# A two-layer decoder's state space scan: two states on the partition halves, 64-column state sums, and copied step sizes

## The reference

```python
xz = x @ W_in;  xc, z = split(xz)
xc = silu(causal_conv4(xc) + conv_b)
dt_r, Bm, Cm = split(xc @ W_xproj)            # 16, 16, 16 columns
dt = softplus(dt_r @ W_dt + b_dt)
A = -exp(A_log)                               # 512 channels x 16 states
h_t = h_{t-1} * exp(dt_t * A) + (dt_t * xc_t) * Bm_t
y_t = sum_n h_t[:, n] * Cm_t[n]
y = (y + xc * D) * silu(z)
out = y @ W_out                               # added to the residual
```

## Time and profile before

| what | us |
|---|---|
| median of three runs | 3156.37 (3152.83 to 3161.01) |
| the profiled execution's own time | 3155.42 |
| its span, first to last instruction | 3153.9 |
| Mamba stage: first scan to last finish | 39.77 to 1019.4 |
| VectorE busy in 38 to 1018 us | 917.3 of 980 |
| TensorE busy in the same stretch | 851.6 of 980 |
| mean granted TensorE clock, whole span | 0.956 |

### The profile page before, as it was taken

How to read it: one execution, slowest core, us unless ns; L and a number is a source line. 1 busy time by engine, 2 the same in 40 slices (tenths; PEclk the granted TensorE clock), 3 DMA queues, 4 the chain that set the end, 5 groups by cost and what they waited for, 6 DMA issues and landing times. The chain is left out here.

```text
span 3153.9 us, 41299 instructions
## 1 busy us (share of the span) xinstructions
PE 2825.9 (90%) x14210; PEld 1841.1 (58%) x14210; DVE 2063.7 (65%) x3705; ACT 1471.9 (47%) x2768; POOL 1510.8 (48%) x1192
## 2 busy tenths in 40 slices
PE   6898988988986877899999999988878999999998
PEld 2343343433432664555556555556657888888887
DVE  7899999999999744577777777658862222222221
ACT  5667666676763400366666666645531111111111
POOL 5788787888886544133433343256751111111111
PEclk8999999999999878999999999989988999999999
DMA  7135044053150054213232222211116665566662
GB/s 237 48 114 162 21 143 144 18 162 121 41 172 0 28 166 150 82 32 82 60 88 58 67 59 59 65 44 35 51 66 211 203 190 184 184 189 202 205 189 61
DMA packets 283854, 346.31 MB, mean 110 GB/s; under 512 B 85787, under 2 KB 238551, under 8 KB 283591
## 3 DMA queue, kind: packets, MB, share of 16 engines
q1 hardware_dynamic: 260399, 310.17, 31.8%
q0 software_dynamic: 16704, 27.21, 3.7%
q10 hardware_dynamic: 6544, 6.30, 0.7%
HBM read 234.69 MB, written 107.95 MB: 109 GB/s over the span
## 5 line engine op out<-in xcount | busy, mean ns | idle before, releaser
L542 POOL TENSOR_TENSOR mb_drive<-mb_dtx,mb_b_rep 128x1024 f32<-128x1024 f32 x255 | 597.2, 2358 | 181.9 <-DVE mb_pD L439 89.0
L853 PE MATMUL mb_pY<-mb_hc,ident 128*128 128x512 f32 x1024 | 501.6, 615 | 57.1 <-DVE mb_hc L456 56.8
L1986 DVE TENSOR_REDUCE at_nm_of<-at_pS 128x2 f32<-128x256 f32 (+1 forms) x630 | 383.3, 635 | 113.0 <-PE at_pS L1976 57.4
L3161 POOL DMA_INDIRECT out<-et_y,et_to x71 | 112.0, 1577 | 661.0 <-DVE et_y L3215 406.7
L3205 DVE TENSOR_TENSOR et_mT<-et_silu,et_pU 128x512 f32<-128x512 f32 (+1 forms) x160 | 100.2, 627 | 470.7 <-ACT et_silu L3176 470.7
L3176 ACT ACTIVATE et_silu<-et_pG 128x512 f32<-128x512 f32 (+1 forms) x160 | 87.9, 549 | 652.6 <-PE et_pU L3237 652.6
L853 PEld LDWEIGHTS mb_pY<-mb_hc,ident 128*128 128x128 f32 x1024 | 189.7, 194 | 328.7 <-issue 184.4
L598 ACT ACTIVATE mb_pD<-mb_dt,mb_a_neg 128x512 f32<-128x512 f32 x384 | 259.6, 688 | 154.6 <-DVE mb_hc L456 143.0
L439 DVE TENSOR_TENSOR_SCAN mb_pD<-mb_pD,mb_drive 128x1024 f32<-128x1024 f32 x128 | 292.8, 2288 | 43.0 <-ACT mb_pD L596 40.5
L445 DVE TENSOR_TENSOR_SCAN mb_pD<-mb_pD,mb_carried,mb_drive 128x512 f32<-128x512 f32 x256 | 313.8, 1269 | 8.0 <-ACT mb_pD L598 8.0
L456 DVE TENSOR_TENSOR mb_hc<-mb_pD,mb_c_rep 128x1024 f32<-128x1024 f32 x256 | 308.1, 1204 | 1.0 <-PE mb_pY L853 1.0
(11 more groups left out here) (491 smaller groups left out, 4986.2 us busy)
## 6 DMA issues: line engine op xcount, KB each, us to landing
t_wg<-in_t_wgT SPq DMA_DIRECT2D x40, 1024.0 KB, 6.1
t_wu<-in_t_wuT SPq DMA_DIRECT2D x40, 1024.0 KB, 9.0
t_wd<-in_t_wdT SPq DMA_DIRECT2D x40, 1024.0 KB, 11.3
mb_b_rep<-mb_rows SPq DMA_DIRECT2D x64, 512.0 KB, 5.6
mb_c_rep<-mb_rows SPq DMA_DIRECT2D x64, 512.0 KB, 4.9
t_h_sorted<-blank SPq DMA_DIRECT2D x6, 4160.0 KB, 19.9
t_h_sorted<-blank SPq DMA_DIRECT2D x18, 1170.0 KB, 6.3
t_h_sorted<-blank SPq DMA_DIRECT2D x12, 1040.0 KB, 5.8
```

Of the source, the lines that this page charges most:

```text
L542: nc.gpsimd.tensor_tensor(drive[G % RINGS][:, :, :], dtx[:, m, :].unsqueeze(1).to_broadcast([P, 2, CH]), b_rep[:, 2 * j:2 * j + 2, :], ALU ...
L853: last = nc.tensor.matmul(pY[:, :], K.ident[:, :], hc[G % RINGS][:, k, :], start=False, stop=(j == PAIRS - 1 and k == 1))
L1986: nc.vector.tensor_reduce(nm_of[t % 2][:, w0 // 512, sides[0]:sides[0] + m, qb], score_bank(t, k)[:, 0:m * w].rearrange("p (a w) -> p a w" ...
```

## The change

Channel halves and states change places. A tensor's partitions 0 to 63 now hold state 2j and partitions 64 to 127 state 2j+1, and the two slots k of the free dimension hold the channels k*64 to k*64+63 of tile m. An item has the same 256 rows of 512 as before.

- The step sizes are needed in that layout on both partition halves, so SyncE copies `dt` and `dtx` after GpSimd has made them to `dt2` and `dtx2` (three buffers, `TWINS = 3`), eight transfers of 64 x 512 (128 KB) for each tile (`twins`). Decays read `dt2`, drives read `dtx2`.
- B and C rows are read as two transfers of 64 partitions each (128 KB), each row to one half, and are shared by both slots.
- `state_sum` uses `fold` (128 x 64, two identities one above the other): slot k sums the two halves into PSUM partitions k*64 to k*64+63. The skip term is split in the same way.
- On SyncE the copies of tile 0 stand behind the B and C rows of j = 2, those of tiles 1 and 2 behind j = 7, then `fill_rows`, then those of tile 3.
- GpSimd runs `step_sizes` of the next chunk's tile 0 ahead of the drive of s = 29 and no longer of s = 31.
- `magnitude` on ScalarE waits for the copies in place of the drives. A_log is laid out anew on the host (`twin_rows`).

```diff
+    HP = P // 2
+    TWINS = 3
-        a_neg = sb("a_neg", [P, ME, NST])
+        a_neg = sb("a_neg", [P, ME, 2, PAIRS])
+        fold = sb("fold", [P, HP])
-        b_rep, c_rep = sb("b_rep", [P, NST, CH]), sb("c_rep", [P, NST, CH])
+        dt2, dtx2 = sb("dt2", [P, TWINS, 2, CH]), sb("dtx2", [P, TWINS, 2, CH])
+        b_rep, c_rep = sb("b_rep", [P, PAIRS, CH]), sb("c_rep", [P, PAIRS, CH])
...
+            def twins(ch, m):
+                nth = ch * ME + m
+                q = nth % TWINS
+                for made, to, s_made, s_to, s_used, per in ((dt, dt2, s_dt, s_dt2, s_dec, 2), (dtx, dtx2, s_dtx, s_dtx2, s_drv, 1)):
+                    eng.wait_ge(s_made, nth + 1)
+                    if nth >= TWINS:
+                        eng.wait_ge(s_used, (nth - TWINS + 1) * PAIRS * per)
+                    for k in range(2):
+                        for h in range(2):
+                            eng.dma_start(to[h * HP:(h + 1) * HP, q, k, :], made[k * HP:(k + 1) * HP, m, :]).then_inc(s_to[q], 16)
...
-                    eng.dma_start(b_rep[:, 2 * j:2 * j + 2, :], rows_dram[ch % 2][2 * j:2 * j + 2, :].partition_broadcast(P)).then_inc(s_b[j], 16)
+                    for h in range(2):
+                        eng.dma_start(b_rep[h * HP:(h + 1) * HP, j, :], rows_dram[ch % 2][2 * j + h, :].partition_broadcast(HP)).then_inc(s_b[j], 16)
...
+                    if j == 2:
+                        twins(ch, 0)
+                twins(ch, 1)
+                twins(ch, 2)
                 fill_rows(K, eng, K.h1_sorted, ch, NCH, s_fill)
+                twins(ch, 3)
...
+        def drive_of(unit, ch, m, j, r):
+            return unit.tensor_tensor(drive[r][:, :, :], dtx2[:, (ch * ME + m) % TWINS, :, :],
+                                      b_rep[:, j, :].unsqueeze(1).to_broadcast([P, 2, CH]), ALU.mult)
...
-                nc.vector.tensor_tensor(hc[r][:, :, :], pD[r][:, :, :], c_rep[:, 2 * j:2 * j + 2, :], ALU.mult).then_inc(s_hc, 1)
+                nc.vector.tensor_tensor(hc[r][:, :, :], pD[r][:, :, :], c_rep[:, j, :].unsqueeze(1).to_broadcast([P, 2, CH]), ALU.mult).then_inc(s_hc, 1)
...
+            nc.vector.tensor_tensor(fold[:, :], K.ident[:, 0:HP], K.ident[:, HP:P], ALU.add).then_inc(s_fold, 1)
...
-                    if s == 31 and ch + 1 < NCH:
+                    if s == 29 and ch + 1 < NCH:
                         step_sizes(eng, nc.gpsimd, ch + 1, 0)
...
                 if ch > 0:
-                    eng.wait_ge(s_drv, (ch - 1) * ITEMS + (m + 1) * PAIRS)
+                    twin_made(eng, s_dt2, (ch - 1) * ME + m)
+                    twin_made(eng, s_dtx2, (ch - 1) * ME + m)
...
-                    nc.tensor.matmul(pY[:, :], skip[:, m, :], xc(ch, m), start=True, stop=False)
+                    for k in range(2):
+                        nc.tensor.matmul(pY[k * HP:(k + 1) * HP, :], skip[:, m, k * HP:(k + 1) * HP], xc(ch, m), start=True, stop=False,
+                                         skip_group_check=True)
                 eng.wait_ge(s_hc, G + 1)
                 for k in range(2):
-                    last = nc.tensor.matmul(pY[:, :], K.ident[:, :], hc[G % RINGS][:, k, :], start=False, stop=(j == PAIRS - 1 and k == 1))
+                    last = nc.tensor.matmul(pY[k * HP:(k + 1) * HP, :], fold[:, :], hc[G % RINGS][:, k, :], start=False, stop=(j == PAIRS - 1),
+                                            skip_group_check=True)
```

More of the change, by code:

```diff
@@ L288, in mamba @@
             sem(n) for n in ("dec", "drv", "scan", "keep", "hc", "y", "fin", "rows", "fill"))
+        s_dt2, s_dtx2 = [sem(f"dt2_{q}") for q in range(TWINS)], [sem(f"dtx2_{q}") for q in range(TWINS)]
+        s_fold = sem("fold")
         s_b = [sem(f"b{j}") for j in range(PAIRS)]
@@ L321, in _ @@
                 loads.append((dst[:, :], io[name].rearrange("(m p) -> p m", p=P)))
-            loads += [(a_neg[:, :, :], io["mb_A_log"].rearrange("(m p) n -> p m n", p=P)),
+            loads += [(a_neg[:, :, :, :].rearrange("p m k j -> p (m k j)"), io["mb_A_log"]),
                       (w_x[:, :, :], io["mb_w_x"].rearrange("(m p) n -> p m n", p=P)),
@@ L349, in _, with twin_made @@
             for j in range(PAIRS):
-                eng.wait_ge(s_b[j], 16 * NCH)
-                eng.wait_ge(s_c[j], 16 * NCH)
-        ALL_IN = 16 * 7
+                eng.wait_ge(s_b[j], 32 * NCH)
+                eng.wait_ge(s_c[j], 32 * NCH)
+            for q in range(TWINS):
+                uses = len(range(q, NCH * ME, TWINS))
+                eng.wait_ge(s_dt2[q], 64 * uses)
+                eng.wait_ge(s_dtx2[q], 64 * uses)
+        ALL_IN = 16 * 7
+        def twin_made(eng, s_to, nth):
+            eng.wait_ge(s_to[nth % TWINS], 64 * (nth // TWINS + 1))
+        def drive_of(unit, ch, m, j, r):
+            return unit.tensor_tensor(drive[r][:, :, :], dtx2[:, (ch * ME + m) % TWINS, :, :],
+                                      b_rep[:, j, :].unsqueeze(1).to_broadcast([P, 2, CH]), ALU.mult)
         def normalise(eng, unit, ch):
@@ L426, in first_drive @@
             def first_drive():
[L427 to L430, removed]
+                twin_made(eng, s_dtx2, 0)
+                eng.wait_ge(s_b[0], 32)
+                drive_of(nc.vector, 0, 0, 0, 0).then_inc(s_drv, 1)
             def scans(G):
@@ L538, in drives @@
                 if m == 0:
-                    eng.wait_ge(s_b[j], 16 * (ch + 1))
+                    eng.wait_ge(s_b[j], 32 * (ch + 1))
                 if G >= RINGS:
                     eng.wait_ge(s_scan, 2 * (G - RINGS) + 2)
-                nc.gpsimd.tensor_tensor(drive[G % RINGS][:, :, :], dtx[:, m, :].unsqueeze(1).to_broadcast([P, 2, CH]),
-                                        b_rep[:, 2 * j:2 * j + 2, :], ALU.mult).then_inc(s_drv, 1)
+                drive_of(nc.gpsimd, ch, m, j, G % RINGS).then_inc(s_drv, 1)
             inverse_deviation(0)
@@ L582, in decay @@
                 r = G % RINGS
-                scale = a_neg[:, m, 2 * j + k:2 * j + k + 1]
+                scale = a_neg[:, m, k, j:j + 1]
+                step = dt2[:, (ch * ME + m) % TWINS, k, :]
                 if k == 0:
                     if j == 0:
-                        eng.wait_ge(s_dt, ch * ME + m + 1)
+                        twin_made(eng, s_dt2, ch * ME + m)
                     if G == RINGS - 1:
@@ L871, in _ @@
             eng.wait_ge(s_diag, ME * TAPS + ME)
+            eng.wait_ge(s_fold, 1)
             for i in range(NCH):
@@ L3295, in layout, with twin_rows @@
     same = lambda n: np.ascontiguousarray(np.asarray(inputs[n]))
+    def twin_rows(n):
+        a = np.asarray(inputs[n])
+        a = a.reshape(-1, 2, P // 2, a.shape[1] // 2, 2)
+        return np.ascontiguousarray(np.transpose(a, (4, 2, 0, 1, 3)).reshape(P, -1))
     return {
```

26 lines of the change are left out of this document (13 added, 13 removed).

## The result

Against the kernel before, over eight runs of each on one chip, the changed kernel takes 1.0034 times as long, 95% interval 1.0023 to 1.0045 (medians 3165.1 and 3154.6 us, +10.6 us; forecast +12.5 us). The profiled execution's own time is 3171.3 us, the longest of the eight. Beside each stands the stage itself in the one profiled execution of the run. In the kernel before its first scan starts at 39.77 us and its last `finish` at 1018.70 us; after, at 47.13 and 1029.95 us (+11.3).

What follows compares the result with a forecast made beforehand. VectorE was taken as the bound, its 893 us of scans and weighings unchanged, only some 62 us of waits to be won. The terms 17.9 + 4.2 - 9.6 = +12.5 us on 3155.4 gave 3168 us, range 3152 to 3187.

Steps and rivals of the forecast that it cites:

- the likeliest case: Whole kernel: GpSimd's stall at chunk ends and a later start outweigh the relief of TensorE; 3168 us, chance 0.50.
- relief and stall about cancel: Rival, same mechanisms at the kind ends: sums save 0.8 us or more, start costs 3; +8.8 us, 3164 us, chance 0.22.
- Part 1, the size for one sum: TensorE's state sum: two halves side by side take 1.1 to 1.3 us in place of 1.91, saving 0.6.
- Part 1, what reaches the end: VectorE's waits: 8.4 of 11.2 us in `finish` and 1.2 us in chunk 0 are won, -9.6 us in all.
- Part 2: Step sizes at s = 29: GpSimd stands still for ScalarE's logarithm, drives queue behind it; +17.9 us over seven boundaries.
- Part 3, the start: First copies of dt and dtx, covered by nothing: scan 3 starts at 55.9 us against 51.82, +4.2 us (3 to 6).
- Part 3, the boundaries: Copies at chunk boundaries land at 405.2 to 407.4 us, before item 32's drive at 408.5: covered, 1 to 3 us to spare.
- the halves don't overlap: Rival on TensorE's state sums: halving gives nothing and the switches cost some 5 us; 3183 us, chance 0.06.
- Faster: Rival: TensorE's relief moves ScalarE's whole chain, most decay waits go, 40 of 62 us recovered; 3138 us, chance 0.12.
- The lower clock: Rival: TensorE, idle for longer, drops to the 1.2 GHz level, a late matmul at each boundary; 3195 us, chance 0.05.
- Late copies: Rival: copies land late at chunk boundaries, 3 us at each of seven; 3189 us, chance 0.05.

Runs made afterwards that it cites:

- a_s31: The changed kernel with the step sizes back at s = 31: ratio 1.0000 to the kernel before, last finish at 1019.61 us.
- b_s29: The kernel before with only the next chunk's tile 0 step sizes moved from s = 31 to s = 29: ratio 1.0069, last finish at 1038.66 us.
- a_wide: The changed kernel with full-width state sums again, step sizes at s = 29: ratio 1.0073 to the kernel before, last finish at 1046.66 us.
- a_wide31: The changed kernel with full-width state sums and step sizes back at s = 31: ratio 1.0045 to the kernel before, last finish at 1030.32 us.
- m_rows: The changed kernel with step sizes at s = 31 and each pair of B or C rows read by one transfer: ratio 1.1238 to the kernel before.
- a_warm: The changed kernel with step sizes at s = 31 and a zero-weight matmul ahead of each state sum: ratio 1.0133 to the kernel before, last finish 1059.35 us.

## Why the prediction was right, and where it was not

The time came out within 2 us of the forecast (+10.6 against +12.5), and the mechanisms of the likeliest case are there: the stall of GpSimd ahead of drive 29, the overlapping halves, the late start. That it came so close is in part luck, since errors in the terms cancel. The interval of the ratio, +7 to +14 us, also holds the +8.8 of *relief and stall about cancel*; what speaks against that case are its terms, not the time. The steps:

- **Part 1, the size for one sum.** 1.1 to 1.3 us and a saving of 0.6 were forecast. A sum takes 1.01. Beside a convolution, which is slowed by 0.19, the saving is 3.43 - 2.92 = 0.51 us, and beside PROJ it is 0.91. The 0.1 to 0.2 us for each change of form were right. The base of 1.91 us was not a plain one: between convolutions the same sum took 1.72. Next to PROJ the kernel before paid for a change of form already.
- **Part 1, what reaches the end.** -9.6 us was forecast, and -10.7 measured at s = 31. The waits in `finish` gave 9.1 us of it (12.9 to 3.8) where 8.4 was forecast. The 5.33 us wait of chunk 0 became 5.01, not 4.1. The sum took VectorE's pitch as 3.49 us, from durations; by their starts, two scans without a wait are 3.32 us apart in an even chunk (395.26 and 398.58 in the kernel after). TensorE's 3.43 us for a state sum and a convolution is above that, so it could fall behind in dense stretches, and the forecast saw that only in `finish`.
- **Part 2.** +17.9 us forecast; +18.9 measured alone, 17.7 of it in the waits from scan 29 on. The reading of the earlier trace rows held at both kinds of chunk end; scan 29 waited 4.1 to 5.5 us, where 2.8 to 5 was said. Together with the rest of the change it cost 10.3 us. The step that failed is that the terms were added as if each were free of the others. At the chunk ends the stall swallows waits that are there without it: 22.4 us in a_s31, against 17.7 in the kernel before.
- **Part 3, the start.** +4.2 us (3 to 6) forecast, and scan 0 at 43 to 45 us; it came at 47.13, scan 3 7.7 us later than before, the first `finish` 6.8 (84.14 to 90.93). The mis-sized term is SyncE's issue, taken at 0.43 us. Twenty issues take 12.7 us (31.31 to 44.00) and not 8.6: 4.1 us.
- **Part 3, the boundaries.** Forecast as covered, and they were.

By the path before, b_s29, a_wide, after, the terms are +20.0 (1.05 of it ahead of the first scan), +8.0 and -16.7, together +11.3. By the path before, a_wide31, a_s31, after they are +11.6, -10.7 and +10.3. The forecast had +17.9 for the move, +4.2 for the copies and -9.6 for the halves. So the sum was closer than its terms on either path: by the first the start was too small by 3 to 4 us and part 1's gain too small by 7; by the second the copies were too small by 7 and the move too large by 8.

Of the rivals, *the halves don't overlap* is ruled out by the state sums. *Faster*, by way of ScalarE, is ruled out too: 21.1 us of decay waits remain at s = 29, but 39.0 at s = 31, where 40.5 were before, so part 1 did not take them away; the stall only renamed them. *Relief and stall about cancel* wanted 0.8 us or more from each sum and 3 us at the start; beside a convolution a sum gave 0.51, and the first scan came 7.4 us later. *The lower clock* came about in the clock (0.84) and, in the time, only at the places shown. *Late copies* did not occur.

## What to carry to other kernels

When a queue runs in order, moving a producer earlier makes everything behind it wait for the producer's own last input; look up when that input is ready before moving the call, and count the queued items at its price. Terms that fall into the same wait do not add: measure a part both with and without the other. A releaser that the trace names can be one that merely ended at that moment; check that the waiting instruction uses it.

## What was not expected of the hardware

- Transfers whose slowest dimension has size 2 ran on 2.1 of 16 engines at 50 GB/s (m_rows, 33 to 50 us), against 204 GB/s for the rows as two transfers to 64 partitions each, with the copies in flight beside them (a_s31).
- SyncE's issue took 0.60 us for most 64-partition transfers of 128 KB (kernel after), and 0.32 to 0.43 us for most 128-partition ones of 512 KB (kernel before), though these too took up to 1.05 us at the start.
- Matmuls on the two 64-column halves run beside each other in fp32: four records in 1.01 us where full width took 1.72. They also do when one half has more to do (six records in 1.86 us, a_warm) or when the work beside is a matmul of 48 columns (PROJ and a state sum in 2.85 us where it was 3.76). Entering or leaving the form costs 0.14 to 0.19 us.
